# Query and key projections of the last attention from three fp32r products, with a weight load and eight normalisations moved back

## The chip, the cores and the metric

One core of a Trainium2 chip runs the kernel. The metric is the device time of one execution in microseconds (us). A profiled execution also leaves a trace: TensorE (PE for matmuls, PEld for its weight loads), VectorE (DVE), ScalarE (ACT), GpSimd (POOL), SyncE (SP, which here only issues DMAs) and the DMA queues.

## The reference

Four layers of attention and feed-forward work on 2 x 1024 rows of 256 values. The change is in the last attention, in which 1024 + 64 keys per batch (the rows and 64 context rows, both normalised) serve 1024 queries:

```python
xn = layer_norm(x, ln_media_w, ln_media_b)       # 64 context rows
zn = layer_norm(latents, ln_lat_w, ln_lat_b)     # 1024 rows
q = (zn @ Wq)...                                 # 8 heads of 64
kv_in = jnp.concatenate([xn, zn], axis=1)
k = (kv_in @ Wk)...
v = (kv_in @ Wv)...
sim = jnp.einsum('bhqd,bhfd->bhqf', q * scale, k)
alphas = jax.nn.softmax(sim, axis=-1)
out = jnp.einsum('bhqf,bhfd->bhqd', alphas, v)
...
return out @ Wout
```

## The kernel before

The attention (`pe_xattn3`, `act_xattn3`, `dve_xattn3`, `pool_xattn3`, `sp_xattn3`, one function for each engine, each a fixed order written out by hand, with semaphores between them) runs over 16 blocks `G`. A block is one pair of heads and one half (512) of the queries of a batch: batch `G // 8`, pair `G // 2 % 4`, half `G % 2`; keys and values are shared by the two blocks of a pair `n = G // 2`. A block has nine steps `j`, one for each tile of 128 keys (the ninth has the 64 context keys).

In step `j` TensorE makes the scores of tile `j` (four fp32r matmuls: the keys' and queries' high parts, and then both low parts with the negated maxima as one more row), at steps 3, 6 and 8 the products of three tiles with the values (fp32), then a *side*, and last two *rough* tiles of the next block, fp32r scores of which only the row maxima are kept. ScalarE weighs each tile (`act_weigh3`, exp of 128x1024, L2423), GpSimd adds the weights up (`pool_sum3`, 128x1024 from two operands in SBUF, L2470 and L2473), and divides the block before at its step 7 (`pool_divide3`, L2453). VectorE reduces the rough tiles (L2373), makes the reciprocals in quarters (`quarters3`, `dve_divisors3`, L2445; none in block 0), and at step 8 the next block's maxima (`dve_maxima3`, L2378 and two small operations in L2380).

A side is a piece of the preparation of later blocks, all through PSUM bank 7: `q` at step 1 projects the queries of block `G + 2`; `k` at steps 2, 4 and 5 of even blocks projects the keys of the next pair (512, 512 and 64 columns), `v` in odd blocks its values; `s` at step 3 sums the weights over the keys; `m` at step 8 transposes the next block's negated maxima (L2242), and TensorE goes on to the next block behind it; `o` is the output projection. Behind a `q` or `k` side ScalarE copies the result as fp32r high parts (L2280 or L2265, and again for the other half of the partitions), and VectorE subtracts them from PSUM for the low parts (L2302). TensorE's next side waits for those (`s_lo3`), since it writes the same bank.

A rough tile waits until the one two before it has been reduced (`s_ar`). Names: `XT` holds the transposed normalised rows in fp32 (2 x 2048 columns), `x3_CT` the context's, `x3_WQ`, `x3_WK`, `x3_WV` the weights from `oW` on; `XN` is the normalised rows' place from 4096 on, free in the attention until `dve_norm` (L173) fills it with the normalised output, the next stage's input. `s_mi` counts the sides that TensorE has made, `s_mo` what ScalarE has kept, `s_x` finished row tiles, `s_xn` normalised ones. All matmuls are issued by `mm`, L152.

Of the kernel before, what the change touches and what calls it, by code (L numbers as in the profile page):

```python
# [6 lines left out]
ALU = mybir.AluOpType  # L7
# [71 lines left out]
def build(nc, d, out):  # L79
    with ExitStack() as ctx:  # L80
# [2076 lines left out]
        x3_MX, x3_M1, x3_NM = view(o + 15872, 4, 2, 3), view(o + 15896, 4, 2), view(o + 15904, 4, 65)  # L2157
        x3_SM, x3_RC = view(oAW + 3072, 512), view(oAW + 3584, 512)
        x3_OE = [view(oW + 8448 + 1024 * p, 1024) for p in range(3)] + [view(oW + 15360, 1024)]
        s_mi, s_mo, s_lo3 = sem("side_made"), sem("side_kept"), sem("low_parts")  # L2160
        s_one = sem("ones_rows")
        s_am, s_ar = sem("rough_scores"), sem("rough_maxima")
# [46 lines left out]
        def pe_side3(e, s):  # L2209
# [12 lines left out]
            if kind in "kv":  # L2222
                b, p, rows = a // 4, a % 4, 128 if c < 2 else 64
                src = XT[:, :, 1024 * b + 512 * c:1024 * b + 512 * c + 512] if c < 2 else x3_CT[:, :, 64 * b:64 * b + 64]
            if kind == "k":
                n = 512 if c < 2 else 64
                for k in range(2):
                    m = mm(e, psum[:, bk, 0:n], x3_WK[:, k, 128 * p:128 * p + 128], src[:, k, :], k == 0, k == 1)
# [20 lines left out]
            else:  # L2249
                e.wait_ge(s_on, 40 + a + 1 + (c if a == 15 else 0))  # L2250
                for y, t in enumerate(tiles3(a, c)):
                    for p in range(4):
                        m = mm(e, psum[:, bk, 256 * y:256 * y + 256], x3_OE[p][:, 128 * (t % 8):128 * (t % 8) + 128],
                               x3_WO[:, p, :], p == 0, p == 3)
            m.then_inc(s_mi, 1)

        def act_side3(e, s):
            kind, a, c = s
# [215 lines left out]
            m.then_inc(s_pa, 1)  # L2474

        def sp_xattn3(e):
            e.wait_ge(s_xt, 57)
            e.wait_ge(s_x, 96)
            e.dma_start(view(oW + 12288, 3072), d["w3b"][:, 8192:8192 + 3072]).then_inc(s_w3, 16)
            e.wait_ge(s_sc, 48 + 144)  # L2480
            e.dma_start(view(oW + 4096, 4096), d["w3b"][:, 0:4096]).then_inc(s_wm, 16)
            e.wait_ge(s_x, 112)
            e.dma_start(view(oW + 8192, 4096), d["w3b"][:, 4096:8192]).then_inc(s_wm, 16)
# [52 lines left out]
        def act_xattn3(e):  # L2536
            e.wait_ge(s_tp, 57)
            for k in range(2):
                m = e.activation(x3_CT[:, k, :], psum[:, 4, 128 * k:128 * k + 128], ACT.Identity,
                                 bias=sml("mbc")[:, k:k + 1], scale=sml("mwc")[:, k:k + 1])  # L2540
            m.then_inc(s_xt, 1)
            for s in FIRST3[6:]:
                act_side3(e, s)
            for G in range(16):
                for j in range(9):
                    act_weigh3(e, G, j)
                    if j == 8:
                        act_values3(e, G)
                    if side3(G, j):
                        act_side3(e, side3(G, j))  # L2550
                    for i in next_turn3(G, j):
                        act_turn(e, 7, i)
            act_side3(e, ("s", 15, 0))
            for i in range(4, 8):
                act_turn(e, 7, i)

        def dve_xattn3(e):
# [9 lines left out]
            for G in range(16):  # L2567
                for j in range(9):
                    if j == 8 and G + 1 < 16:
                        dve_maxima3(e, G + 1)  # L2570
                    if side3(G, j):
                        dve_side3(e, side3(G, j))
                    if j == 8 and G + 2 < 16:
                        dve_rough3(e, G + 2, 0)
                    if j < 8 and G + 1 < 16:
                        for i in rough_step3(j):
                            dve_rough3(e, G + 1, i)
                    if G:
                        for i in quarters3(G, j):
                            dve_divisors3(e, G - 1, i)  # L2580
                    if (G, j) == (15, 4):
                        dve_divide3(e, 14, slice(0, 512))
                    if G in (9, 11) and 2 <= j <= 5:
                        dve_norm(e, 113 + 2 * (G - 9) + j - 1, 2 * (G - 9) + j - 2)
            dve_side3(e, ("o", 14, 0))
            for t in range(8, 10):
                dve_norm(e, 113 + t + 1, t)
# [527 lines left out]
```

## Time and profile before

| | |
|---|---|
| three timed executions | 1929.12, 1933.93, 1934.39 us, median 1933.93 |
| profiled execution, its time | 1927.72 us |
| span of its instructions | 1925.9 us |
| busy, share of the span | PE 86%, PEld 58%, DVE 56%, ACT 47%, POOL 44% |
| TensorE's granted clock, mean | 0.922 of 2.4 GHz |

The last attention's 16 blocks run from 1208 to about 1720 us of the span. A block with `k` sides takes some 32 us, one with `v` sides some 31.

### The profile page before, as it was taken

To read this page: it belongs to the slowest core of one execution; us is meant where nothing else is said; L and a number is where in the kernel's file an instruction comes from. 1 tells how busy PE (TensorE), PEld (TensorE's weight loads), DVE (VectorE), ACT (ScalarE), POOL (GpSimd) and SP (SyncE) were. 2 spreads that over 40 slices of the span, in tenths; PEclk is the share of its full clock that TensorE was granted. 3 is DMA by queue.
4 is the path that set the end of the run, shared out by engine and by line. 5 is a ranking of instruction groups with operands and counts; after the bars stand their busy time and mean duration, and the time that the engine had idled before them with its cause. 6 is when DMAs were issued, how large, how long until landed. Compare 5 with 4: busy or idle time off the path is not lost.

```text
span 1925.9 us, 26333 instructions
## 1 busy us (share of the span) xinstructions
PE 1652.5 (86%) x9225; PEld 1115.1 (58%) x9225; DVE 1087.6 (56%) x2204; ACT 904.7 (47%) x1502; POOL 851.3 (44%) x802
## 2 busy tenths in 40 slices
PE   5954999969965999974996887999999999997998
PEld 3444999946844333354994665555555655563674
DVE  4662546576866345442446698556655666544335
ACT  2412445513335888742452665555455355431363
POOL 2053221123478455523004474566665666654206
PEclk9776999979987899986998997899999999997999
DMA  9613233030000000062113000000000000012354
GB/s 364 221 58 106 81 137 131 18 117 1 1 21 1 1 7 6 6 263 92 45 50 104 6 1 33 1 1 1 1 1 1 1 1 1 1 44 96 124 169 133
DMA packets 61881, 117.77 MB, mean 61 GB/s; under 512 B 7247, under 2 KB 50499, under 8 KB 59064
## 3 DMA queue, kind: packets, MB, share of 16 engines
q1 hardware_dynamic: 53688, 95.90, 14.2%
q0 software_dynamic: 8064, 20.19, 3.2%
q8 instruction: 77, 1.26, 0.3%
q14 instruction: 52, 0.43, 0.1%
HBM read 72.26 MB, written 44.89 MB: 61 GB/s over the span
## 4 chain that ended last, share of the span: by engine, by line
PE 66%; DVE 12%; POOL 7%; ACT 5%; issue 5%; DMA 4%; SPq 0%; POOLq 0%; ACTq 0%; DVEq 0%
PE psum L152 61%; POOL arena L1815 2%; DMA arena<-xb 2%; ACT arena L1588 2%; DVE arena L2373 2%; POOL arena L856 2%; DVE rounded L2302 2%; POOL arena L1831 1%; POOL xb L1043 1%; DVE arena L157 1%; DVE arena L2445 1%; PE psum L668 1%; DVE arena L1940 1%; DVE arena L173 1%; DVE arena L2380 1%
## 5 line engine op out<-in xcount | busy, mean ns | idle before, releaser
L152 PE MATMUL psum<-arena 128*128 (+16 forms) x5084 | 1034.1, 439 | 106.4 <-DVE arena L1698 21.1
L152 PEld LDWEIGHTS psum<-arena 128*128 128x128 f32 (+4 forms) x5084 | 584.9, 175 | 435.9 <-issue 289.8
L152 PE MATMUL psum<-rounded 128*128 128x256 f32 (+9 forms) x3072 | 547.4, 344 | 14.4 <-ACT arena L1588 5.3
L152 PEld LDWEIGHTS psum<-rounded 128*128 128x128 f32 (+5 forms) x3072 | 408.3, 186 | 172.2 <-issue 63.4
L2473 POOL TENSOR_TENSOR arena<-arena 128x1024 f32<-128x1024 f32 (+1 forms) x111 | 263.2, 2371 | 130.8 <-ACT arena L2423 127.3
L2373 DVE TENSOR_REDUCE arena<-psum 128x1 f32<-128x512 f32 x256 | 163.8, 682 | 98.3 <-PE psum L152 96.8
L2423 ACT ACTIVATE arena<-psum 128x1024 f32<-128x1024 f32 x144 | 147.3, 1024 | 147.8 <-PE psum L152 147.1
L1588 ACT ACTIVATE arena<-psum,arena 128x1024 f32<-128x1024 f32 (+1 forms) x192 | 156.2, 910 | 32.3 <-PE psum L152 32.1
L1831 POOL TENSOR_TENSOR arena<-arena 128x256 f32<-128x256 f32 x128 | 99.4, 803 | 99.5 <-ACT arena L1588 97.8
L856 POOL DMA_INDIRECT arena<-yb,arena x48 | 45.9, 956 | 210.0 <-DMA yb<-arena 196.5
L1196 POOL DMA_INDIRECT yt<-arena x40 | 39.8, 996 | 182.1 <-DVE arena L1159 176.6
L904 DVE SCALAR_TENSOR_TENSOR rounded<-arena,rounded 128x540 fp32r<-128x540 f32 (+1 forms) x96 | 81.8, 885 | 33.4 <-ACT rounded L1105 32.3
L1099 ACT ACTIVATE arena<-psum,arena 128x540 f32<-128x540 f32 x64 | 45.5, 710 | 106.5 <-PE psum L152 103.7
L162 POOL TENSOR_SCALAR arena<-arena 128x1 f32<-128x1 f32 x89 | 22.2, 249 | 146.7 <-DVE arena L158 120.0
L1714 DVE RECIPROCAL arena<-psum 128x512 f32<-128x512 f32 x16 | 53.7, 3358 | 51.4 <-PE psum L152 51.4
L2302 DVE SCALAR_TENSOR_TENSOR rounded<-psum,rounded 64x512 fp32r<-64x512 f32 (+1 forms) x80 | 47.6, 595 | 61.6 <-ACT rounded L2280 32.6
L1790 DVE SCALAR_TENSOR_TENSOR arena<-psum,arena 128x128 f32<-128x128 f32 x92 | 25.9, 344 | 74.5 <-PE psum L152 74.5
L200 ACT ACTIVATE arena<-psum 128x512 f32<-128x512 f32 x48 | 27.1, 596 | 82.8 <-PE psum L192 82.8
L2445 DVE RECIPROCAL arena<-arena 128x128 f32<-128x128 f32 x64 | 58.9, 936 | 11.9 <-ACT arena L2289 11.6
L192 PE MATMUL psum<-arena 128*128 128x128 f32 x192 | 30.9, 300 | 31.9 <-DVE arena L173 29.6
L2470 POOL TENSOR_TENSOR arena<-arena 128x1024 f32<-128x1024 f32 x16 | 38.1, 2382 | 44.9 <-ACT arena L2423 44.9
L1815 POOL TENSOR_TENSOR arena<-arena 128x20 f32<-128x20 f32 x16 | 56.9, 3556 | 1.3
(262 smaller groups left out, 1837.1 us busy)
## 6 DMA issues: line engine op xcount, KB each, us to landing
arena<-in_w SPq DMA_DIRECT2D x8, 2048.0 KB, 8.7
arena<-xb SPq DMA_DIRECT2D x70, 128.0 KB, 2.3
yb<-arena SPq DMA_DIRECT2D x70, 128.0 KB, 1.8
arena<-in_w1u SPq DMA_DIRECT2D x4, 2048.0 KB, 14.0
xb<-arena SPq DMA_DIRECT2D x3, 2048.0 KB, 16.0
xb<-arena SPq DMA_DIRECT2D x2, 2064.0 KB, 31.6
arena<-xb SPq DMA_DIRECT2D x8, 516.0 KB
yt<-arena SPq DMA_DIRECT2D x2, 2048.0 KB, 15.0
```

The costliest lines, as they stand in the source:

```text
L152: return e.matmul(o, l, r, start=start, stop=stop, skip_group_check=True)
L856: e.indirect_dma_start(dst, None, buf, bass.IndirectOffsetOnAxis(idx[:, col:col + 1], 0)).then_inc(s_gth[s], 16)
L904: e.scalar_tensor_tensor(out=dst, in0=src, scalar=1.0, in1=hi, op0=ALU.mult, op1=ALU.subtract).then_inc(sig, 1)
L1588: e.activation(PT[:, u % 3, 2 * h:2 * h + 2, 0:n], psum[:, bk:bk + 2, 0:n], ACT.Exp, bias=NBD[:, 0:1]).then_inc(s_ae, 1)
L1714: settle(e, dve, e.reciprocal(got(c), psum[:, 6 + c % 2, :]))
L1815: e.tensor_tensor(RSH[:, t % 4, :], RSH[:, t % 4, :], cst("nhalf")[:, 0:1].broadcast_to([128, 20]), ALU.pow).then_inc(s_rh, 1)
L1831: e.tensor_tensor(PT[:, u % 3, 2 * h:2 * h + 2, 0:128], PT[:, u % 3, 2 * h:2 * h + 2, 0:128], bc(cst("caus"), 1, 2), ALU.mult).then_inc(s_ ...
L2302: e.scalar_tensor_tensor(out=lo, in0=psum[r, bk, 0:64 if (kind, c) == ("k", 2) else 512], scalar=1.0, in1=hi, op0=ALU.mult, op1=ALU.subtra ...
L2373: m = e.tensor_reduce(x3_MX[:, t, a, c:c + 1], psum[:, bk, :], AX.X, ALU.max)
L2423: e.activation(x3_P[0:rows, g % 4].rearrange("p a n -> p (a n)"), psum[0:rows, bk:bk + 2, :].rearrange("p a n -> p (a n)"), ACT.Exp, scale ...
L2445: e.reciprocal(x3_RC[:, 128 * i:128 * i + 128], x3_SM[:, 128 * i:128 * i + 128]).then_inc(s_rc3, 1)
L2473: m = e.tensor_tensor(ac, ac, x3_P[0:rows, g % 4], ALU.add)
```

## The change

The queries from block 3 on and the keys from pair 2 on are no longer made by fp32 products (two matmul calls, one for each half of the 256 inner values) but by fp32r ones: rows and weights are split into a high part (the value rounded to fp32r) and a low part (the rest), and for each inner half the products high x high, weight high x row low and weight low x row high are summed, six matmul calls. The values stay fp32.

The parts of rows (one batch at a time, 2 x 1024 columns), weights and context are made in the attention: the high ones by ScalarE in steps 5 and 6 of block 0 and step 5 of block 5, the low ones by VectorE in steps 6 and 7 of both blocks. The rows' parts lie in `XN`'s place, the weights' low part over the fp32 weights, the high part where the next stage's weights `w3b[:, 8192:]` were loaded. So that load is issued only after the last `q` side, and the eight `dve_norm` of blocks 9 and 11 stand in blocks 13 and 14.

```diff
+        x3_XH, x3_XL = rview(4096, 2, 1024), rview(4096 + 2048, 2, 1024)
+        x3_WH, x3_WL = rview(oW + 12288, 2, 2, 512), rview(oW, 2, 2, 512)
+        x3_CH, x3_CL = rview(oW + 14336, 2, 128), rview(oW + 14592, 2, 128)
+        s_hi3, s_lw3 = sem("high_parts"), sem("rest_parts")
...
-            if kind == "k":
+            if kind in "kq" and parted3(s):
+                b, p, h = (a // 4, a % 4, c) if kind == "k" else block3(a)
+                n, w = 512 if (kind, c) != ("k", 2) else 64, 1 if kind == "k" else 0
+                e.wait_ge(s_lw3, 5 + 2 * b)
+                hi, lo = (x3_XH, x3_XL) if n == 512 else (x3_CH, x3_CL)
+                rows = slice(512 * h, 512 * h + 512) if n == 512 else slice(64 * b, 64 * b + 64)
+                i = 0
+                for k in range(2):
+                    for wt, x in ((x3_WH, hi), (x3_WH, lo), (x3_WL, hi)):
+                        m = mm(e, psum[:, bk, 0:n], wt[:, w, k, 128 * p:128 * p + 128], x[:, k, rows], i == 0, i == 5)
+                        i += 1
+            elif kind == "k":
...
+        def parted3(s):
+
+            return s[1] >= (3 if s[0] == "q" else 2)
+
+        def act_parts3(e, b):
+
+            if b:
+                e.wait_ge(s_mi, max(SIDE3_AT["q", 7, 0], SIDE3_AT["k", 3, 2]) + 1)
+            else:
+                e.wait_ge(s_xt, 57)
+                e.wait_ge(s_tp, 56)
+            for k in range(2):
+                e.activation(x3_XH[:, k, :], XT[:, k, 1024 * b:1024 * b + 1024], ACT.Copy).then_inc(s_hi3, 1)
+
+        def act_weight_parts3(e):
+            for w in range(2):
+                e.activation(x3_WH[:, w].rearrange("p k n -> p (k n)"), view(oW + 1024 * w, 1024), ACT.Copy).then_inc(s_hi3, 1)
+            e.activation(x3_CH.rearrange("p k n -> p (k n)"), x3_CT.rearrange("p k n -> p (k n)"), ACT.Copy).then_inc(s_hi3, 1)
+
+        def dve_parts3(e, b, k):
+
+            e.wait_ge(s_hi3, 3 + 2 * b + k + 1)
+            if b and k == 0:
+                e.wait_ge(s_mi, max(SIDE3_AT["q", 7, 0], SIDE3_AT["k", 3, 2]) + 1)
+            e.scalar_tensor_tensor(out=x3_XL[:, k, :], in0=XT[:, k, 1024 * b:1024 * b + 1024], scalar=1.0, in1=x3_XH[:, k, :],
+                                   op0=ALU.mult, op1=ALU.subtract).then_inc(s_lw3, 1)
+
+        def dve_weight_parts3(e, w):
+
+            e.wait_ge(s_hi3, w + 1)
+            e.wait_ge(s_mi, max(SIDE3_AT["k", 1, 2], SIDE3_AT["q", 2, 0]) + 1)
+            e.scalar_tensor_tensor(out=x3_WL[:, w].rearrange("p k n -> p (k n)"), in0=view(oW + 1024 * w, 1024), scalar=1.0,
+                                   in1=x3_WH[:, w].rearrange("p k n -> p (k n)"), op0=ALU.mult,
+                                   op1=ALU.subtract).then_inc(s_lw3, 1)
+            if w:
+                e.wait_ge(s_hi3, 3)
+                e.scalar_tensor_tensor(out=x3_CL.rearrange("p k n -> p (k n)"), in0=x3_CT.rearrange("p k n -> p (k n)"),
+                                       scalar=1.0, in1=x3_CH.rearrange("p k n -> p (k n)"), op0=ALU.mult,
+                                       op1=ALU.subtract).then_inc(s_lw3, 1)
...
         def sp_xattn3(e):
-            e.wait_ge(s_xt, 57)
-            e.wait_ge(s_x, 96)
+            e.wait_ge(s_mi, max(SIDE3_AT["q", 15, 0], SIDE3_AT["k", 7, 2]) + 1)
             e.dma_start(view(oW + 12288, 3072), d["w3b"][:, 8192:8192 + 3072]).then_inc(s_w3, 16)
...
+                    if (G, j) in ((0, 6), (5, 5)):
+                        act_parts3(e, G // 5)
+                    if (G, j) == (0, 5):
+                        act_weight_parts3(e)
...
-                    if G in (9, 11) and 2 <= j <= 5:
-                        dve_norm(e, 113 + 2 * (G - 9) + j - 1, 2 * (G - 9) + j - 2)
+                    if G in (0, 5) and j in (6, 7):
+                        dve_parts3(e, G // 5, j - 6)
+                    if G == 0 and j in (6, 7):
+                        dve_weight_parts3(e, j - 6)
+                    if G in (13, 14) and 4 <= j <= 7:
+                        if (G, j) == (13, 4):
+                            e.wait_ge(s_mi, max(SIDE3_AT["q", 15, 0], SIDE3_AT["k", 7, 2]) + 1)
+                        dve_norm(e, 113 + 4 * (G - 13) + j - 3, 4 * (G - 13) + j - 4)
```

## Rows read from the trace of the kernel before

**Rows 1.** Page, part 4: the chain that ended last, by engine.

```profile
PE 66%; DVE 12%; POOL 7%; ACT 5%; issue 5%; DMA 4%; SPq 0%; POOLq 0%; ACTq 0%; DVEq 0%
```

**Rows 2.** Table by stretch, block 5: us, busy PE, PEld, DVE, ACT, POOL, clock, DMA, GB/s.

```profile
1367.00:1398.00 31.00, 30.09 (x149) 18.08 (x149) 17.85 (x28) 14.49 (x19) 20.32 (x11) 1.00 0.00 1
```

**Rows 3.** The chain in order of time behind a query side: start, us, what.

```profile
1309.80 0.60 ACT rounded L2280
1310.43 0.68 DVE rounded L2302
1311.14 0.70 DVE rounded L2302
```

**Rows 4.** Timeline of PEld, fp32 side, then fp32r run: start, us, count, idle before.

```profile
1244.88 0.19 PEld L152 LDWEIGHTS psum<-arena 128*128 128x128 f32 x1
1245.31 0.19 PEld L152 LDWEIGHTS psum<-arena 128*128 128x128 f32 x1 [0.24 <-issue]
...
1242.78 1.82 PEld L152 LDWEIGHTS psum<-rounded 65*128 65x128 f32 x8
```

**Rows 5.** Timeline at step 5 of block 0: the 64-column key side.

```profile
1229.65 0.66 PE L152 MATMUL psum<-arena 128*128 128x64 f32 x4 [0.74 <-DVE rounded L2302]
...
1230.37 0.19 PEld L152 LDWEIGHTS psum<-rounded 128*128 128x128 f32 x1 [0.20 <-DVE arena L2373]
```

**Rows 6.** Timeline of steps 5 to 8 of block 0.

```profile
1231.49 0.54 ACT L2269 ACTIVATE rounded<-rounded 64x64 fp32r<-64x64 f32 x2
1232.43 1.03 ACT L2423 ACTIVATE arena<-psum 128x1024 f32<-128x1024 f32 x1 [0.41 <-PE psum L152]
...
1235.59 2.67 DVE L2373 TENSOR_REDUCE arena<-psum 128x1 f32<-128x512 f32 x4 [2.54 <-PE psum L152]
...
1237.85 4.85 POOL L2473 TENSOR_TENSOR arena<-arena 128x1024 f32<-128x1024 f32 x2 [1.76 <-ACT arena L2423]
...
1238.51 1.81 DVE L2380 TENSOR_SCALAR arena<-arena 128x4 f32<-128x4 f32 x2
...
1241.17 0.65 PE L2242 MATMUL psum<-arena 128*65 128x128 f32 x4
```

**Rows 7.** Groups by form, whole span: count, busy us, mean ns, idle before.

```profile
L901 ACT ACTIVATE rounded<-arena 128x1024 fp32r<-128x1024 f32 x32 | 32.8, 1061 | 0.0
...
L904 DVE SCALAR_TENSOR_TENSOR rounded<-arena,rounded 128x1024 fp32r<-128x1024 f32 x32 | 38.1, 1216 | 0.0
```

**Rows 8.** Timelines, ends of blocks 5 and 14.

```profile
1393.21 0.94 DVE L2445 RECIPROCAL arena<-arena 128x128 f32<-128x128 f32 x1
...
1394.27 2.36 POOL L2473 TENSOR_TENSOR arena<-arena 128x1024 f32<-128x1024 f32 x1 [1.57 <-ACT arena L2423]
...
1395.54 1.19 DVE L2380 TENSOR_SCALAR arena<-arena 128x4 f32<-128x4 f32 x2
...
1397.58 0.54 PE L2242 MATMUL psum<-arena 128*65 128x128 f32 x3
...
1681.39 7.40 POOL L2473 TENSOR_TENSOR arena<-arena 128x1024 f32<-128x1024 f32 x3
...
1690.46 0.62 PE L2242 MATMUL psum<-arena 128*65 128x128 f32 x4 [0.85 <-DVE arena L2380]
```

**Rows 9.** One line's instructions: ns least/median/most, first and last start.

```profile
L173 DVE TENSOR_SCALAR arena<-arena x10: 315/410/448, 1513.1 to 1719.8; 128x256 f32<-128x256 f32 x10
...
L2380 DVE TENSOR_SCALAR arena<-arena x32: 157/395/1736, 1206.1 to 1689.1; 128x4 f32<-128x4 f32 x32
...
L1719 DVE SCALAR_TENSOR_TENSOR arena<-arena x16: 692/1225/1293, 652.6 to 839.9; 128x512 f32<-128x512 f32 x16
```

**Rows 10.** Table by stretch, slow stretches (columns as rows 2).

```profile
1204.25:1214.50 10.25, 8.07 (x26) 6.58 (x26) 5.09 (x10) 2.13 (x3) 3.41 (x3) 0.50 0.01 2
...
1501.20:1504.60 3.40, 3.40 (x11) 2.82 (x11) 1.40 (x3) 1.04 (x2) 2.90 (x7) 0.50 0.00 0
```

**Rows 11.** DMA issues: KB each, median us from issue to landing.

```profile
arena<-in_w3b SPq DMA_DIRECT2D x1, 1536.0 KB, 6.2
```

## The prediction

> **What bounds the kernel now.** I read the chain that ended last first: TensorE carries two thirds of the span [rows 1], so a change in the last attention is worth what it takes off or adds to TensorE's own order of work there. Then the table by stretch: in a block TensorE is busy 30.1 of 31 us at full clock, VectorE, ScalarE and GpSimd between 14.5 and 20.3 [rows 2]. TensorE sets the pace, and the others have 11 to 16 us of room per block as a sum. Room as a sum is not room at every point, so third I read the chain and the timeline through a block. TensorE waits at two kinds of place. After a query or key side it waits for ScalarE's copy (0.60) and VectorE's two low parts (0.68, 0.70) before it may reuse bank 7: 0.73 us of idle [rows 3]. And at step 8 it must transpose the negated maxima (`m`), which VectorE makes last in the block. That second place has almost no room: in block 0 VectorE ends the maxima at 1240.32 and TensorE comes at 1241.17 [rows 6]; in block 5 at 1396.73 against 1397.58 [rows 8]; in block 14 TensorE already waits 0.85 us [rows 8].
>
> **What the parts give.** Thirteen `q` sides (blocks 3 to 15) and twelve 512-column `k` sides (pairs 2 to 7) change from two fp32 products to six fp32r ones; six 64-column `k` sides likewise. An fp32 product shows as two matmuls, and their weight loads start 0.43 us apart (1244.88, 1245.31): four of them are 1.72 us. Eight fp32r weight loads beside 512-column matmuls last 1.82 us, so (1.82 - 0.19)/7 = 0.233 us apart [rows 4]; six are 1.40. The side gets 0.32 us shorter, and since the copy and the low parts follow its end, the 0.73 us of idle stays and the gain passes on: 25 x 0.32 = **-8.0 us**. The Trainium skill (FP8 and Floating Point Precision, TensorE Precision Notes) has true fp32 in 4 passes; with one pass for each fp32r product that would be 4 against 3 passes of the same length, 1.72 to 1.29, and 25 x 0.43 = -10.8 us as an estimate from that page; the weight-load spacing above, 0.233 and not 0.215, speaks against the full step, and I take the measured one.
>
> The 64-column sides get longer: four fp32 matmuls last 0.66 us in all, at a spacing of about 0.11, and six end 0.22 us later. But behind them TensorE waits for VectorE's reductions anyway, until 1230.37, where the four ended their issue at about 1230.15 [rows 5]. So 0; if that cover is gone, 6 x 0.22 = +1.3.
>
> **What the making of the parts costs.** Prices: ScalarE 128x1024 to fp32r 1.06 us, VectorE 128x1024 from two SBUF operands 1.22 [rows 7]; the context's 256 columns I put at 0.4 and 0.5. Per half of the rows 2.1 us on ScalarE and 2.4 on VectorE; for weights and context 2.1 + 0.4 and 2.4 + 0.5. As sums they fit in the room. Their place is steps 5 to 7 of blocks 0 and 5, directly ahead of the maxima in VectorE's queue. There they meet GpSimd: it adds up the weights in 128x1024 operations of 2.37 us. A tiny VectorE operation on SBUF (128x4) takes 0.16 us, but 1.74 at worst; that is the one in block 0 which starts at 1238.51 while GpSimd's sum is under way [rows 6, 9]. L1719, with two SBUF operands, takes 0.69 at least and 1.23 in the median, beside a busy GpSimd [rows 9]. I conclude that such an operation waits for the GpSimd operation under way, and the next GpSimd operation for it.
>
> *Block 0.* ScalarE is free at 1232.03, makes the weights' and the context's high parts until 1234.6, so exp 6 (from 1232.43 before) ends at 1235.6, the rows' high parts at 1236.7 and 1237.7, exp 7 at 1238.7, exp 8 at 1239.8. These delays alone cost TensorE nothing: its last values before `m`, at 1241.17, need exp 8, and take about 1 us [rows 6]. GpSimd sums exp 6 from 1235.7 to 1238.1. VectorE has reduced two of its four tiles at 1236.9, waits for GpSimd until 1238.1, makes rows part 1 until 1239.3; GpSimd's next sum runs to 1241.7; weights part 1 to 1242.9, two reductions to 1244.2, during which GpSimd's last sum starts and runs to 1245.2; then rows part 2, weights part 2 and context, 2.9 us, to 1248.1, the maxima 0.5: 1248.6. TensorE stands at `m` from 1241.17, and behind it in its queue stand the scores of block 1, so ScalarE and GpSimd run dry too: **+7.4 us**. TensorE's own new wait, for the parts at `q` 3, stands behind this one (the maxima come after all parts in VectorE's queue) and is never the last. Without any wait for GpSimd VectorE would end at 1243.7: +2.5, the lower bound.
>
> *Block 5.* ScalarE's two high parts push exp 6 back by some 1.1 us, which nobody waits for. No weights, but one reciprocal at step 6 ends at 1394.15; rows part 1 starts just before GpSimd's sum (1394.27) and ends at 1395.4, reductions 1396.7, GpSimd's sum 1395.4 to 1397.7, rows part 2 to 1398.9, then GpSimd's division (1.26) has the turn to 1400.2 and the maxima end at about 1400.4, against 1397.58 when TensorE comes [rows 8]: **+2.8**; 0.6 without the waits, 5.2 if another sum comes between.
>
> *The norms.* Each is 0.41 us [rows 9], eight of them. In blocks 9 and 11 they stood at steps 2 to 5, where VectorE had room: taking them away gives 0. Block 13 has block 5's pattern, so on block 5's clock [rows 8]: the norm of step 6 goes ahead of the sum, which then runs to 1396.9, the norm of step 7 behind it to 1397.2, the division to 1398.5 and the maxima to 1398.8, against 1397.58: **+1.2**, 0 at the least. In block 14 three sums follow each other without a pause from 1681.39 (7.40 us) [rows 8]; the norm of step 6 is ready at 1686.9 and waits to 1688.8, the last reductions end at 1690.1, the reciprocal at 1691.1, norm and division at 1692.7, the maxima at 1692.9 instead of 1690.31: **+2.5**, 0.7 at the least. They are still in time for the next stage's transposes.
>
> *The clock.* After the halts ahead of block 0 TensorE's granted clock was 0.50 (1.2 GHz) for 10.25 us, and for 3.4 us at the end of block 8 [rows 10]. In such a stretch TensorE does half the work: 3.4 us cost 1.7, and the 10.25 us, with 8.07 busy, some 4. For the halt in block 0 I take 2.3 (bounds 0 and 4), for block 5 0.8 (0 to 1.7), nothing for the shorter ones in 13 and 14: **+3.1**.
>
> *The weight load.* 1536 KB landed in 6.2 us [rows 11]; now it is issued after `q` 15, early in block 13 and over 60 us before the attention's end, behind which its reader, the next stage, starts. On SP's queue only the two loads behind it follow, and they wait for the end of the attention. 0; if it were late, up to 6.
>
> **Sum.** -8.0 + 7.4 + 2.8 + 1.2 + 2.5 + 3.1 = **+9.0 us**. Against the profiled execution, 1925.9 of span and 1.8 around it, that is 1934.9 and 1936.7. The profiled execution was 6.2 below the median of the three runs (1933.93); I add the 9.0 to the median: **1942.9**. Less than 0.3%, 5.8 us, I count as no change.
>
> **Rivals.**
> 1. *The parts don't meet GpSimd* (0.25). VectorE's new operations run at their own length beside the sums. For it: L1719's median is some half a us over its least, not two; against it, GpSimd's operations beside L1719 are short, and the 1.74 us is plain. Then -8.0 + 2.5 + 0.6 + 0 + 0.7 + 0.8 = -3.4: 1930.5, no change. The Trainium skill (SBUF — State Buffer, Who interferes with whom) has it that whoever of the two starts first holds a shared port pair for the whole instruction, also against a VectorE operation with two SBUF inputs; by that rule, with which the 1.74 us agrees, this rival would fall.
> 2. *The maxima are hardly late, and the gain stands: faster* (0.14). Place: step 8 of blocks 0 and 5. If VectorE drains its reductions, which are spaced by TensorE's matmuls, in the gaps, and the maxima come under 2.2 us late over all four blocks, the gain of 8.0 beats 5.8; with 1 us in all, -7.0: 1926.9. If the six products ran at 0.215, -10.8 and it holds up to 5 us of lateness. Against it: block 0 alone has 2.5 us at the least, on durations that are measured.
> 3. *More turns are lost* (0.16). At blocks 5 and 13 the second of the maxima's two small operations loses to GpSimd's last sum, 2.4 us each, and the clock stays low longer after block 0 (+1.7): +9.0 + 6.5 = 1949.4. For it: in block 14 exactly that second operation lasted until the division's end.
>
> **How the numbers follow.** Main case 0.45, rivals 0.25, 0.14, 0.16. The main case's own range, from the bounds of the halts and the clock, is +4 to +13: 1938 to 1947, with 0.06 of its chance below +5.8. Slower: 0.39 + 0.16 = 0.55. No change: 0.06 and 0.22 of rival 1 = 0.28. Faster: rival 2's 0.14 and 0.03 of rival 1 = 0.17. The range takes in rival 1 and most of rival 3, and leaves out rival 2: 1928 to 1950.
>
> **What would show it.** In the changed kernel's profile: six matmuls a side at 0.23 us; side to next side 0.3 us shorter in odd and even blocks; VectorE's new operations in blocks 0 and 5 longer than 1.22 us, and ending with GpSimd's sums; TensorE idle at `m` by some 7 us in block 0, 3 in block 5, 1 to 3 in 13 and 14; a granted clock of 0.5 after block 0. If `m` of block 1 comes within 3 us of its old place, rival 1 is right; if the sides don't shorten, the first term is wrong.

## The result, and the profile after

| | kernel before | changed kernel |
|---|---|---|
| median, us (8 runs each) | 1928.55 (1924.53 to 1934.39) | 1942.19 (1937.54 to 1944.45) |
| profiled execution, its time and span | 1927.72, 1925.9 | 1937.65, 1935.8 |
| mean granted clock | 0.922 | 0.917 |
| attention, first `m` to last `m` | 1206.88 to 1690.46: 483.6 | 1203.51 to 1700.20: 496.7 |

The ratio is 1.0069, 95% interval 1.0054 to 1.0085: slower by some 13 us (10 to 16). Three executions of the whole series, 6 to 30% longer at a lower granted clock, count in no ratio. The attention alone became 13.1 us longer. The span grew by 9.9 only, because this execution came to the attention 3.4 us earlier than the one before did; the change touches nothing there. It is also among the two shortest of the changed kernel's eight, with a mean granted clock of 0.917 where the other seven have 0.913 to 0.915, so a usual execution may spend some us more at half speed than the one read here.

The chain by engine, against [rows 1]: TensorE lost two points and VectorE won two, so more of the end is set by waits for VectorE.

```profile
PE 64%; DVE 14%; POOL 7%; issue 5%; ACT 5%; DMA 4%; SPq 0%; POOLq 0%; ACTq 0%; DVEq 0%
```

Where the sides are, the gain is there. The chain behind a query side (start, us, what) has the same lengths as [rows 3]; the 22 fp32r weight loads of a stretch with such a side are 0.225 us apart, against 0.43 for fp32 [rows 4].

```profile
1344.90 0.60 ACT rounded L2335
1345.50 0.02 issue
1345.53 0.68 DVE rounded L2357
1346.21 0.03 issue
1346.24 0.70 DVE rounded L2357
```

```profile
1340.88 4.93 PEld L152 LDWEIGHTS psum<-rounded 128*128 128x128 f32 x22
```

From `m` to `m`, an even block with three such sides is 1.0 us shorter (block 2: 32.59 to 31.55) and an odd one with one side 0.35 (block 3: 30.43 to 30.07). That is 0.33 to 0.35 a side.

The loss of block 0 is in VectorE's and GpSimd's timelines (start, us, engine, line, what; now L2296 and L2303 make low parts, L2428 reduces, L2435 ends the maxima, L2528 is GpSimd's sum):

```profile
1233.61 2.05 DVE L2296 SCALAR_TENSOR_TENSOR rounded<-arena,rounded 128x1024 fp32r<-128x1024 f32 x1
1235.59 3.37 DVE L2303 SCALAR_TENSOR_TENSOR rounded<-arena,rounded 128x1024 fp32r<-128x1024 f32 x1
1238.89 1.28 DVE L2428 TENSOR_REDUCE arena<-psum 128x1 f32<-128x512 f32 x2
1240.09 2.16 DVE L2296 SCALAR_TENSOR_TENSOR rounded<-arena,rounded 128x1024 fp32r<-128x1024 f32 x1
1242.17 1.21 DVE L2303 SCALAR_TENSOR_TENSOR rounded<-arena,rounded 128x1024 fp32r<-128x1024 f32 x1
1243.30 0.41 DVE L2308 SCALAR_TENSOR_TENSOR rounded<-arena,rounded 128x256 fp32r<-128x256 f32 x1
...
1243.84 0.24 DVE L2435 TENSOR_SCALAR arena<-arena 128x4 f32<-128x4 f32 x2
```

```profile
1232.19 2.39 POOL L2528 TENSOR_TENSOR arena<-arena 128x1024 f32<-128x1024 f32 x1 [1.90 <-ACT arena L2478]
1235.00 6.16 POOL L2528 TENSOR_TENSOR arena<-arena 128x1024 f32<-128x1024 f32 x2 [0.41 <-ACT arena L2478]
```

```profile
1244.22 1.09 PE L2257 MATMUL psum<-arena 128*65 128x128 f32 x4 [6.29 <-DVE arena L2435]
...
1403.57 0.62 PE L2257 MATMUL psum<-arena 128*65 128x128 f32 x4 [2.24 <-DVE arena L2435]
...
1700.20 1.09 PE L2257 MATMUL psum<-arena 128*65 128x128 f32 x4 [3.01 <-DVE arena L2435]
```

Read the first two together. GpSimd's sum ends at 1232.19 + 2.39 = 1234.58, and L2296 ends 1.08 us behind that. L2303 starts at 1235.59 and lasts 3.37 us: the next sum has the turn first, for its 2.4 us, though it was ready at 1235.00 only. The second L2296 ends 1.09 us behind the end of the two sums, 1241.16. The last L2303, with no sum beside it, takes 1.21. So one such operation costs 1.1 to 1.2 us plus what is left of a sum, or a whole one; and the sums, two in 6.16 us instead of 4.85 [rows 6], wait as well. In block 5 the same, on a smaller scale, and there GpSimd's division (L2508) is spread over 2.24 us and L2435's two small operations over 1.10:

```profile
1397.75 1.16 DVE L2296 SCALAR_TENSOR_TENSOR rounded<-arena,rounded 128x1024 fp32r<-128x1024 f32 x1
...
1400.02 2.18 DVE L2296 SCALAR_TENSOR_TENSOR rounded<-arena,rounded 128x1024 fp32r<-128x1024 f32 x1
...
1402.33 1.10 DVE L2435 TENSOR_SCALAR arena<-arena 128x4 f32<-128x4 f32 x2
```

```profile
1397.96 3.16 POOL L2528 TENSOR_TENSOR arena<-arena 128x1024 f32<-128x1024 f32 x1 [1.00 <-ACT arena L2478]
1401.09 2.24 POOL L2508 TENSOR_TENSOR arena<-arena 128x512 f32<-128x512 f32 x1
```

In block 14 two of the norms take 2.2 us, beside four sums in a row; a norm alone takes 0.31. TensorE's idle at `m` there went from 0.85 [rows 8] to 3.01:

```profile
1686.80 2.21 DVE L173 TENSOR_SCALAR arena<-arena 128x256 f32<-128x256 f32 x1
...
1694.43 2.13 DVE L173 TENSOR_SCALAR arena<-arena 128x256 f32<-128x256 f32 x1
...
1698.53 0.31 DVE L173 TENSOR_SCALAR arena<-arena 128x256 f32<-128x256 f32 x1
```

```profile
1686.47 9.94 POOL L2528 TENSOR_TENSOR arena<-arena 128x1024 f32<-128x1024 f32 x4 [0.83 <-ACT arena L2478]
```

What the halts don't explain is the clock. Table by stretch (us, busy PE, PEld, DVE, ACT, POOL, clock, DMA, GB/s) for three stretches at 0.50 (1.2 GHz):

```profile
1241.90:1252.10 10.20, 7.88 (x25) 6.75 (x26) 4.82 (x10) 2.39 (x3) 0.00 (x0) 0.50 0.01 2
1405.80:1409.20 3.40, 3.40 (x9) 2.63 (x9) 1.29 (x2) 1.52 (x2) 0.00 (x0) 0.50 0.00 0
1699.30:1706.10 6.80, 5.88 (x15) 4.36 (x16) 1.45 (x3) 2.61 (x3) 2.97 (x2) 0.50 0.00 0
```

The first begins in block 0's halt, as put, the third in block 14's; the second follows block 5's. Four more of 3.4 us, at 1426.3, 1439.9, 1491.1 and 1511.6, stand in blocks 6 to 9, where no halt is new; in these blocks there was one before, at 1501.2 [rows 10].

All of it by blocks (change in length from `m` to `m`, us; halt is how much later `m` comes for want of the maxima, of which 6.3, 2.24, 0.51 and 2.16 show as new idle at `m`; clock is what is left when 0.33 to 0.35 a side and the halt are taken off):

| block | change | sides | halt | clock | at 0.50, before and after |
|---|---|---|---|---|---|
| 0 | +6.4 | 0 | +6.3 | +0.1 | 7.6, 10.0 |
| 1 | +3.3 | -0.35 | | +3.7 | 0, 8.0 |
| 2, 3, 4 | -2.4 | -2.35 | | 0 | 0, 0 |
| 5 | +2.0 | -0.35 | +2.35 | 0 | 0, 0 |
| 6 | +2.2 | -1.0 | | +3.2 | 0, 6.8 |
| 7 | +1.2 | -0.35 | | +1.6 | 0, 3.4 |
| 8 | +0.6 | -1.0 | | +1.6 | 0, 3.4 |
| 9 to 12 | -2.6 | -2.7 | | 0 | 3.4, 3.4 |
| 13 | +0.3 | -0.35 | +0.6 | 0 | 0, 0 |
| 14 | +2.1 | 0 | +2.1 | 0 | 0, 0.9 |
| sum | +13.1 | -8.4 | +11.4 | +10.2 | |

### The profile page after: what moved, and what is told of

Read it like the earlier page. It is cut to its first block, busy times and chain, and to the rows that moved or that the text cites. A ratio compares the mean times of both kernels' runs of the same rounds, so it can differ in the third digit from the quotient of the medians.

```text
span 1935.8 us, 26493 instructions
## 1 busy us (share of the span) xinstructions
PE 1652.5 (85%) x9287; PEld 1131.8 (58%) x9287; DVE 1102.0 (57%) x2211; ACT 910.8 (47%) x1509; POOL 856.2 (44%) x802
## 4 chain that ended last, share of the span: by engine, by line
PE 64%; DVE 14%; POOL 7%; issue 5%; ACT 5%; DMA 4%; SPq 0%; POOLq 0%; ACTq 0%; DVEq 0%
PE psum L152 60%; DVE arena L2428 2%; ACT arena L1588 2%; POOL arena L1815 2%; DMA arena<-xb 2%; POOL arena L856 2%; DVE rounded L2357 2%; POOL xb L1043 1%; POOL arena L1831 1%; DVE arena L157 1%; DVE arena L173 1%; DVE arena L2500 1%; DVE arena L2435 1%; PE psum L668 1%; DVE arena L1940 1%
## 5 line engine op out<-in xcount | busy, mean ns | idle before, releaser
L152 PE MATMUL psum<-arena 128*128 128x128 f32 (+13 forms) x4960 | 980.7, 435 | 96.1 <-DVE arena L1698 18.8
L152 PEld LDWEIGHTS psum<-arena 128*128 128x128 f32 (+3 forms) x4960 | 562.6, 174 | 406.9 <-issue 280.0
L152 PE MATMUL psum<-rounded 128*128 128x270 f32 (+9 forms) x3258 | 581.9, 345 | 23.2 <-DVE rounded L2357 8.8
L152 PEld LDWEIGHTS psum<-rounded 128*128 128x128 f32 (+3 forms) x3258 | 446.4, 188 | 182.9 <-ACT arena L1588 56.1
L2528 POOL TENSOR_TENSOR arena<-arena 128x1024 f32<-128x1024 f32 (+1 forms) x111 | 265.1, 2388 | 127.2 <-ACT arena L2478 124.2
L2428 DVE TENSOR_REDUCE arena<-psum 128x1 f32<-128x512 f32 x256 | 164.0, 683 | 100.3 <-PE psum L152 98.8
L2478 ACT ACTIVATE arena<-psum 128x1024 f32<-128x1024 f32 x144 | 147.3, 1024 | 150.7 <-PE psum L152 150.0
L173 DVE TENSOR_SCALAR arena<-arena 128x256 f32<-128x256 f32 x128 | 54.7, 449 | 7.1 <-POOL arena L169 3.5
```

What stands on the lines that cost most here:

```text
L152: return e.matmul(o, l, r, start=start, stop=stop, skip_group_check=True)
L173: e.tensor_scalar(xn(t), src(t), MV[:, t, 0:1], RS[:, t:t + 1], ALU.subtract, ALU.mult).then_inc(s_xn, 1)
L2428: m = e.tensor_reduce(x3_MX[:, t, a, c:c + 1], psum[:, bk, :], AX.X, ALU.max)
L2478: e.activation(x3_P[0:rows, g % 4].rearrange("p a n -> p (a n)"), psum[0:rows, bk:bk + 2, :].rearrange("p a n -> p (a n)"), ACT.Exp, scale ...
L2528: m = e.tensor_tensor(ac, ac, x3_P[0:rows, g % 4], ALU.add)
```

## The experiments

The ratio of each is to runs of the kernel before on the same chip. Two chips of three (the runs from `e5_spread` to `e8_fp32_short`, and the last two) take some 280 us instead of 236 behind the attention in every profile taken there, and the kernel before has medians of 1973.05 and 1972.4 on them; so times are compared by ratios, and blocks by their own lengths. Lines of code are cut to the core.

### The norms alone

```diff
-                    if G in (9, 11) and 2 <= j <= 5:
-                        dve_norm(...)
+                    if G in (13, 14) and 4 <= j <= 7:
+                        dve_norm(...)
```

> The kernel before, with only the eight normalisations moved from blocks 9 and 11 to steps 4 to 7 of blocks 13 and 14. Theory A (whatever delays the maxima delays TensorE, and VectorE's operations on SBUF wait for GpSimd's sums): block 13 longer by 0.6 us, block 14 by 2.1, as in the changed kernel; the time +2.7 us, ratio 1.0014. Theory B (the normalisations are hidden, blocks 13 and 14 of the changed kernel are longer for another reason): 0.0.

Measured: 1.0023 (1.0010 to 1.0036). Block 13 +0.56, block 14 +2.13, every other block 0.0. The stretch at 0.50 behind block 14 is 6.8 us long instead of 3.4, and what follows the last `m` took 1.4 more, 236.8 us for 235.4. So the norms cost 2.7 us of halt in their new places. Whether the 1.4 goes with the longer stretch isn't shown: the changed kernel has the same 6.8 us there and takes 235.6 behind it, and `e9_spread_again`, with 3.4, takes 236.0.

### The parts without the new products

```diff
-                    for wt, x in ((x3_WH, hi), (x3_WH, lo), (x3_WL, hi)): ...
+                    m = mm(e, psum[:, bk, 0:n], wf[:, w, k, ...], xf[:, k, :], k == 0, k == 1)
```

> The changed kernel with all parts made, at their places and with their waits, but the query and key sides back to fp32 products of the unsplit rows and weights (the weights' low part is written over their high part, so that the fp32 weights stay). Theory A (halts from the making of the parts, and the slower clock in blocks 1 and 6 to 8 follows from them): the halts stay, 6.3 us in block 0 and 2.2 in block 5, slow clock behind them stays, and the 8 us of the sides are given back: before +19 to +21 us, ratio 1.0100 to 1.0109. Theory C (the slow clock of blocks 6 to 8 comes from the fp32r sides themselves): halts stay, no slow clock in blocks 6 to 8, before +15, ratio 1.0077.

Measured: 1.0090 (1.0070 to 1.0110). Blocks 0, 1, 5, 13 and 14 got longer by 6.38, 3.68, 2.33, 0.58 and 2.13; the others kept their lengths, but for block 9, which lost its stretch at 0.50. TensorE's idle at `m` is that of the changed kernel (6.29 there):

```profile
1246.19 1.09 PE L2256 MATMUL psum<-arena 128*65 128x128 f32 x4 [6.30 <-DVE arena L2434]
```

So the making of the parts with the norms costs 15.1 us in these blocks, 11.4 of it a later `m`, whatever product reads them. The ratio can't tell theory A from theory C, since its interval is 13.5 to 21.2 us; the attention of the profiled execution, 13.5 longer, is on the side of C. What surprised: with all the halts, nothing in blocks 2 to 13 ran at 0.50, though TensorE idled 2.24 us at the end of block 5 as in the changed kernel.

### The products without the low parts

```diff
-                e.wait_ge(s_lw3, 5 + 2 * b)
+                e.wait_ge(s_hi3, 5 + 2 * b)
...
-                    for wt, x in ((x3_WH, hi), (x3_WH, lo), (x3_WL, hi)):
+                    for wt, x in ((x3_WH, hi), (x3_WH, hi), (x3_WH, hi)):
...
-                        dve_parts3(e, G // 5, j - 6)
-                        dve_weight_parts3(e, j - 6)
```

> The changed kernel without the low parts: VectorE makes none of them, and the six products of a side read the high parts in their place; the high parts, the late load and the moved normalisations stay. Theory A: no halt in blocks 0 and 5, so no slow clock behind them; -8.0 us from the sides, +2.7 from the normalisations: before -5.3 us, ratio 0.9972. Theory C (slow clock from the fp32r sides): slow stretches in blocks 6 to 8 stay at 6.4 us of loss, before +1, ratio 1.0006.

Measured: 0.9993 (0.9981 to 1.0005). No halt in blocks 0 and 5; even blocks -1.0, odd ones -0.35, as in the changed kernel. ScalarE's high parts cost TensorE nothing. But block 4 has a new stretch at 0.50 (1352.6), 1.6 us: -8.4 + 2.7 + 1.6 = -4.1, and the attention is 3.8 shorter. The ratio gives -1.3 (-3.7 to +1.0). That shuts out theory A's -5.3 and comes near theory C's +1; but the stretches that C put in blocks 6 to 8 didn't come, only the one in block 4.

### GpSimd's sums cut where the parts stand

```diff
+            if G in (0, 5) and j >= 6:
+                e.tensor_tensor(ac[:, :, 0:1], ac[:, :, 0:1], x3_P[0:rows, g % 4, :, 0:1], ALU.add)
```

> The changed kernel with GpSimd's sums at steps 6, 7 and 8 of blocks 0 and 5 cut to one column (left out but for that; a 1 is added to the sums of these two blocks so that their reciprocals stay finite). Theory A (VectorE's operations with two SBUF operands wait for GpSimd's): each takes its own 1.2 us, the halt in block 0 falls from 6.3 us to about 2.5, the one in block 5 from 2.2 to at most 0.3; with less slow clock behind them the time falls from the changed kernel's before +13.4 to about before +4, ratio 1.0020. Theory D (the number of VectorE's operations alone makes the lateness): the halts stay, ratio 1.0069.

Measured: 1.0053 (1.0035 to 1.0070). VectorE's same operations in block 0, with nothing long beside them on GpSimd, and TensorE behind them:

```profile
1239.99 1.23 DVE L2296 SCALAR_TENSOR_TENSOR rounded<-arena,rounded 128x1024 fp32r<-128x1024 f32 x1
1241.13 1.22 DVE L2303 SCALAR_TENSOR_TENSOR rounded<-arena,rounded 128x1024 fp32r<-128x1024 f32 x1
...
1243.47 1.21 DVE L2296 SCALAR_TENSOR_TENSOR rounded<-arena,rounded 128x1024 fp32r<-128x1024 f32 x1
```

```profile
1246.66 0.62 PE L2257 MATMUL psum<-arena 128*65 128x128 f32 x4 [2.35 <-DVE arena L2438]
```

That is the mechanism: each operation is back at 1.22 us, the halt of block 0 falls from 6.29 to 2.35 (the lower bound of the prediction was 2.5), that of block 5 from 2.24 to 0.46. The 2.35 that is left is the length of the added work itself ahead of the maxima. The time missed the expectation all the same: eight stretches of 3.4 us at 0.50 (1248.3, 1299.5, 1313.2, 1364.4, 1565.7, 1579.4, 1630.6, 1644.3), none of them in blocks 0 and 5, and only the first behind one of these two. This pointed away from the halts as the cause of the clock.

### The parts spread over earlier steps

```diff
+        PARTS_AT3 = {
+            (0, 3): lambda e: (dve_parts3(e, 0, 0), dve_context_part3(e)),
+            (1, 2): lambda e: dve_parts3(e, 0, 1),
+            (1, 3): lambda e: dve_weight_parts3(e, 0),
+            (1, 4): lambda e: dve_weight_parts3(e, 1),
+            (5, 3): lambda e: dve_parts3(e, 1, 0),
+            (5, 4): lambda e: dve_parts3(e, 1, 1)}
...
+                    if G == 13 and 2 <= j <= 5: (norms 0 to 3)
+                    if G == 15 and j < 2: (norms 4 to 7)
```

`q` 3 stays an fp32 side here, since its parts come later; ScalarE makes its parts at steps 2, 3, 5 and 6 of block 0 and 2 and 3 of block 5.

> The changed kernel with the making of the parts and the normalisations spread: VectorE makes one part a step, at steps 3 of block 0, 2 to 4 of block 1 and 3 and 4 of block 5, where TensorE's step is long (query 3 therefore stays fp32, 24 long sides instead of 25), and the normalisations stand at steps 2 to 5 of block 13 and 0 and 1 of block 15. Theory A (only the place ahead of the maxima costs): no halt, no slow clock behind one, -7.7 us, ratio 0.9960. Theory C (fp32r sides bring slow stretches of their own, some 4 us, as the kernel with products only suggests): -3.7 us, ratio 0.9981. If the parts cost wherever they stand: not below 1.0000.

Measured: 1.0008 (0.9997 to 1.0019). Blocks 1, 5, 13 and 14 are late no more (+0.03, -0.28, -0.31, -0.01). Block 0 is 5.0 longer: VectorE at step 3 and TensorE behind it.

```profile
1226.24 2.62 DVE L2296 SCALAR_TENSOR_TENSOR rounded<-arena,rounded 128x1024 fp32r<-128x1024 f32 x1
1228.78 2.57 DVE L2309 SCALAR_TENSOR_TENSOR rounded<-arena,rounded 128x256 fp32r<-128x256 f32 x1
1231.27 1.40 DVE L2358 SCALAR_TENSOR_TENSOR rounded<-psum,rounded 64x512 fp32r<-64x512 f32 x2
```

```profile
1232.72 1.11 PE L152 MATMUL psum<-arena 128*128 128x64 f32 x4 [3.58 <-DVE rounded L2358]
```

The context's part is 0.41 us of work (L2308 above) and took 2.57, a sum of GpSimd's ahead of it. The rows' part ahead of it had lost a turn too, 2.62 us for 1.2. Both stood ahead of step 4's key side's low parts (L2358), and TensorE waited 3.58 us instead of 0.73 for them: 2.85 of the 5.0 us. The rest came with 6.8 us at 0.50 from 1231.8 on. The ratio is where the third expectation had it, but not for its reason: the other parts cost nothing in their places. So room counts up to the next thing that TensorE needs from VectorE, which is a side's low parts as well as `m`.

### The narrow key side one step later, in both kernels

```diff
-            if j in (2, 4, 5) and n + 1 < 8:
-                return ("v" if G % 2 else "k", n + 1, (2, 4, 5).index(j))
+            at = (2, 4, 5) if G % 2 or G == 8 else (2, 4, 6)
+            if j in at and n + 1 < 8:
+                return ("v" if G % 2 else "k", n + 1, at.index(j))
```

In the spread kernel, and in the kernel before:

> The spread kernel, with the 64-column key side at step 6 instead of 5 in blocks 0, 2, 4, 6, 10 and 12. Between the key side of step 4 and this one TensorE then has work, so its 0.73 us of idle at step 5 goes; the narrow side's low parts (0.47 us) come nearer to the maxima. Theory C1 (that idle is what the slow stretches start from, which in the changed kernel begin some 21 us into even blocks): they go too; -1.6 to -4.4 us for the idle and -4 for the clock, ratio 0.9931 to 0.9952. Theory C2 (they have nothing to do with this idle): ratio of the spread kernel less 0.0008 to 0.0023.

> The kernel before with only the 64-column key side at step 6 instead of 5 in six even blocks. No slow stretches there in the kernel before, so the idle alone: -1.6 us (0.73 less 0.47 in each of six blocks) to -4.4 us, ratio 0.9977 to 0.9992.

Measured: 1.0063 (1.0045 to 1.0082) and 1.0064 (1.0049 to 1.0080). Both missed. Block 2 of the second:

```profile
1297.35 2.00 PE L152 MATMUL psum<-rounded 128*128 128x512 f32 x5 [1.46 <-DVE arena L2374]
```

```profile
1298.80:1302.20 3.40, 3.40 (x9) 1.02 (x9) 1.34 (x2) 1.02 (x1) 3.03 (x2) 0.50 0.00 0
```

Ahead of step 5's first rough tile TensorE now idles 1.46 us instead of 0.73: the tile waits for VectorE's reductions, which stand behind the low parts, and the narrow side had been done in that time for nothing. A block with 1.46 lost 1.0 us where the clock held, and 2.6 with a stretch at 0.50 behind it, as here and in blocks 4, 10 and 12. So stretches come in a kernel of fp32 sides as well when these idles are longer. This is the cover that the prediction named for the 64-column sides, seen from its other side.

### An fp32 side as short as the new one

```diff
-                    m = mm(e, psum[:, bk, 0:n], x3_WK[...], src[:, k, :], k == 0, k == 1)
+                    w = 320 if n == 512 and a >= 2 and k else n
+                    m = mm(e, psum[:, bk, 0:w], x3_WK[...], src[:, k, 0:w], k == 0, k == 1)
```

and the same for `q`, in the kernel before. 192 of the 512 columns lack their second product, so this kernel only shows what a shorter side is worth.

> The kernel before, fp32, with the second product of each query side from 3 on and of each long key side from pair 2 on cut to 320 of 512 columns (the rest of that product is left out), which makes a side 1.39 us, as long as six fp32r products. No parts, no moved operations. Theory C3 (slow stretches come with the kind of the products): none in blocks 2 to 8 and 10 to 13, -8.0 us, ratio 0.9958. Theory C4 (they come with the shorter blocks, at another beat): slow stretches there as in the kernel with products only, -4 us, ratio 0.9979.

Measured: 0.9962 (0.9948 to 0.9975), the first clear gain of the series. Even blocks -0.98, odd ones -0.3, and one stretch at 0.50 in blocks 1 to 13 (1628.2, where theory C3 had none). Block 9 has lost its stretch and block 13 has one instead, so the attention's 8.0 us are the sides alone: shorter sides are worth their full 8 us when the products remain fp32.

### The spread kernel, mended, and the changed kernel again

```diff
-            (0, 3): lambda e: (dve_parts3(e, 0, 0), dve_context_part3(e)),
-            (1, 2): lambda e: dve_parts3(e, 0, 1),
+            (0, 6): lambda e: dve_parts3(e, 0, 0),
+            (1, 2): lambda e: (dve_parts3(e, 0, 1), dve_context_part3(e)),
```

(ScalarE's weight parts move to steps 2 and 3 of block 1.) `e10_changed_again` is the changed kernel beside it on the same chip.

> The spread kernel with block 0 mended: there VectorE's rows part and context part at step 3 waited for GpSimd and made the low parts of the key side of step 4 late (3.6 us of idle). Now block 0 has one part, at step 6, and no high part of ScalarE's between; the context's part stands at step 2 of block 1. Theory A: block 0 as long as before, all other blocks as in the spread kernel, -5 us against that kernel's ratio of 1.0008, and less slow clock: ratio 0.997, -4 to -7.7 us. If a part at step 6 of block 0 already makes the maxima late: block 0 longer by 1 to 3 us, ratio 0.998 to 1.000.

> The changed kernel once more, beside the others of this call on their chip. Ratio 1.0069 as before, in its earlier interval of 1.0054 to 1.0085; halts of 6.3 us in block 0 and 2.2 in block 5. Theory C (slow stretches come with the fp32r sides): at least one in blocks 6 to 13 that follows no halt over 1.5 us.

Measured: 0.9997 (0.9982 to 1.0013) and 1.0086 (1.0068 to 1.0105). The mended kernel has no new halt: blocks 0, 1, 5, 13 and 14 changed by +0.08, +0.03, -0.34, -0.33 and 0.00, and the attention takes 480.4 us instead of 483.6. It is 3.2 shorter and not 7.7, because of stretches at 0.50 in blocks 4, 7 and 8 besides the one of block 9. So the blocks came as theory A had them, but the ratio of 0.997 was missed by the clock. The changed kernel, whose ratio came out at the upper end of its first interval, repeated its halts (6.31, 2.25, 3.01) and had 17 us at 0.50 in blocks 2 to 13, not at the same places as the first time (1358.9, 1403.3 for 6.8, 1427.2, 1509.1); two of them, 1427.2 and 1509.1, follow no halt, as its theory C asked.

### What the clock goes by: the kind of product, or the low parts

Both start from the mended kernel. The first makes all parts, and its sides are the short fp32 ones; the second makes no low parts, and its sides are six fp32r products.

```diff
+                for k in range(2):
+                    y = 320 if n == 512 and k else n
+                    m = mm(e, psum[:, bk, 0:y], wf[:, w, k, ...], xf[:, k, 0:y], k == 0, k == 1)
```

```diff
-                    for wt, x in ((x3_WH, hi), (x3_WH, lo), (x3_WL, hi)):
+                    for wt, x in ((x3_WH, hi), (x3_WH, hi), (x3_WH, hi)):
...
-                        PARTS_AT3[G, j](e)
```

> The mended spread kernel with all parts made at the same places, but the query and key sides fp32 again, the second product of each long side cut to 320 of 512 columns (the rest of it left out; the weights' low part is written over their high part): a side as long as six fp32r products, all else the same. Theory C3 (the slow stretches that ate the gain come with fp32r products): none or one in blocks 2 to 13, -7.0 us or more, ratio 0.9955 to 0.9965. Theory C5 (they come with the making of the parts, or with the beat of the blocks): as the mended spread kernel, ratio 0.9997, its interval 0.9982 to 1.0013.

> The mended spread kernel without the low parts: VectorE makes none, all six fp32r products of a side read high parts; the normalisations stand at their hidden places. Theory C3: slow stretches as in the mended spread kernel, three or so of 3.4 us in blocks 2 to 13, ratio 0.9975 to 1.0000. If only the making of the low parts brings them: ratio 0.9955 to 0.9965.

Measured: 0.9964 (0.9948 to 0.9980) and 0.9981 (0.9964 to 0.9997). Blocks 2 to 13 of four kernels in the table by stretch (columns as above, the clock third from the end), in the order `e8_fp32_short`, `e11_spread_fp32_short`, then `e9_spread_again`, `e12_spread_high_only`:

```profile
1272.05:1658.36 386.31, 365.75 (x1651) 213.40 (x1649) 242.53 (x392) 203.67 (x282) 248.33 (x125) 1.00 0.00 1
```

```profile
1267.02:1653.36 386.34, 365.75 (x1651) 213.45 (x1649) 243.64 (x390) 205.42 (x284) 249.92 (x125) 1.00 0.01 5
```

```profile
1268.99:1659.76 390.77, 370.49 (x1711) 225.66 (x1709) 243.55 (x390) 205.42 (x284) 249.86 (x125) 0.98 0.01 5
```

```profile
1268.76:1659.69 390.93, 370.62 (x1710) 225.75 (x1709) 241.47 (x388) 205.44 (x284) 248.16 (x125) 0.98 0.01 5
```

With fp32 sides 386.3, with fp32r sides 390.8 or 390.9, and low parts or none make no difference. The 4.5 us are the clock: 3.4 us at 0.50 in the first two, 13.6 in the last two, which have their stretches at the same four places (1351.9, 1427.0, 1478.2, 1498.6 and 1351.6, 1426.7, 1477.9, 1498.4). The 10.2 us more at half speed cost 4.5. Both expectations of C3 were met. What these runs hold apart is the sides from all the rest, and not the type of the product from the number of products: with fp32r sides the same blocks have 60 matmuls and 60 weight loads more (1711 for 1651, 1709 for 1649), and no run has as many fp32 ones.

Over all the profiled executions, one of each kernel, us at 0.50 in blocks 2 to 13:

| sides | kernels | us |
|---|---|---|
| fp32 | before, e1, e2, e8, e11 | 3.4, 3.4, 0, 3.4, 3.4 |
| fp32r | changed, e3, e4, e5, e9, e10, e12 | 17, 6.8, 23.8, 10.2, 13.6, 17, 13.6 |
| narrow side moved | e6 (fp32r), e7 (fp32) | 20.4, 13.6 |

## Why the prediction was right, and where its sum was off

The time forecast, 1942.9, was met (1942.19), and the forecast of slower too. The difference was forecast as +9.0 and is +13.6 of the medians, +13.1 of the attention. That the level came out to 0.7 us is luck, for two errors met: the median of three that I added to was 5.4 us above the one of eight, 1933.93 against 1928.55, and the sum was some 4.5 too small.

- **The sides, -8.0**: -8.4 measured, 0.33 to 0.35 a side where 0.32 was put, with a spacing of 0.225 for 0.233. The step was right, and the idle behind a side stayed at 0.73. The estimate of -10.8 from the 4 passes that the Trainium skill (FP8 and Floating Point Precision, TensorE Precision Notes) has for true fp32, with fp32r products 0.215 apart, didn't come true: they are 0.225 apart. The 64-column sides cost nothing, as put.
- **Block 0, +7.4**: 6.3, in the order of the working: rows part 1 behind one sum, weights part 1 behind the whole next one (3.37 us), rows part 2 behind the last, the rest free at 1.21. The us between is in the small steps; ScalarE's parts took 1.0 us each, not 1.06, so GpSimd's sums started earlier.
- **Block 5, +2.8**: 2.35, with the division ahead of the maxima, as put.
- **The norms, +1.2 and +2.5**: 0.6 and 2.1 in blocks 13 and 14; `e1_norms_moved` has them alone, with the same 0.56 and 2.13.
- **The weight load, 0**: it landed in 5.9 us and nobody waited.
- **The clock, +3.1**: this is the term that was mis-sized; it measured +10. I had put 2.3 for block 0's halt and 0.8 for block 5's, and nothing elsewhere. Block 0's halt cost 3.8 (10.2 us at 0.50, within my bound of 4), and the same 10.2 us stand there in `e2_parts_only` and `e10_changed_again`. The stretch behind block 5's halt cost 1.6, but that the halt made it isn't shown: with the same idle `e2_parts_only` has none there, and `e10_changed_again` 6.8 us. Another 4.8 come from stretches in blocks 6 to 8 that follow no new halt. My upper bound of the difference, +13, fell just short of what came, and was as near only because the halts came in 2.5 under their terms. Nor is +4 to +13 what my bounds add up to: with every term at its lower bound the sum is -4.2, with every term at its upper one +14.0.

Rival 1, that the parts don't meet GpSimd, falls by the rows of block 0 and by `e4_sums_cut`: the same operations take 1.22 us when the sums are cut. The Trainium skill (SBUF — State Buffer, Who interferes with whom) says that the first of the two to start holds the port pair that they share for the whole instruction and the other blocks fully. The trace agrees where L2296 ends 1.08 and 1.09 us behind a sum's end. Rival 2 falls with 6.3 us of halt in block 0 alone. Rival 3 would have had its extra turns at blocks 5 and 13, where none was lost; the part of it that spoke of a clock low for longer was nearest to what came.

What is shown: of block 0's halt of 6.3 us, 3.9 come from VectorE's SBUF operations and GpSimd's sums taking turns (cutting the sums removes them) and 2.35 from the added work itself; for the norms in blocks 13 and 14 the turns are read from the timeline only. The halts go away when the parts are spread and kept clear of a side's low parts (`e9_spread_again`). Then the change is worth between -3.4 and +2.5 us by its ratio, -3.2 in the profiled attention, and not -8, because of the clock (`e9` against `e11`, which differ in the sides' products alone, and by 1.5 us for each stretch; their chips differ, but `e12`, on the chip of `e11`, has the blocks of `e9`). What stays open is why fp32r sides bring the low clock, and whether it is the type or the number of the products. All that the rows give is the place: in every profile each stretch at 0.50 in blocks 1 to 13 starts 0.5 to 2.6 us behind an idle of TensorE of 0.73 us or more, mostly some 21 us into an even block or 1.5 us into an odd one. Of such idles blocks 2 to 13 have 25, in the kernel before as in `e9` and `e11`, 7 to 14 us apart (once some 20) and then, in each pair of blocks, 30 us without one; the kernel before and `e11` have a stretch behind one of the 25, `e9` behind four. The two chips' ratios of `e9` and `e12`, which have the same blocks, are 0.9997 and 0.9981, so the end effect of the stretches in unprofiled runs is known to some 3 us only. None of the kernels that leave nothing out is shown to be faster than the one before.

## What to carry to other kernels

Room on VectorE is to be counted from one deadline to the next (here a side's low parts, and `m`), and an operation with SBUF operands beside GpSimd's can cost its own length plus nearly one whole GpSimd instruction, even when it is 0.4 us long (here 2.57). Work that looks like the last of a block should be put behind the deadline rather than ahead of it: the same parts and norms that cost 11.4 us of halts brought none when spread. And a saving in TensorE's own work should be measured together with the granted clock of the stretch, since more than half of this one (4.5 of 7.7 us in the profiled executions) went there, without a halt of its own.

## What the runs showed of the hardware

- Of two VectorE operations in a row, the second can lose its turn to a GpSimd operation that became ready while the first ran or waited: 3.37 us for an operation of 1.21.
- A VectorE operation with one tensor operand in SBUF is caught as well: the norms (128x256) took 2.21 and 2.13 us beside the sums, 0.31 alone.
- About a halt of 6.3 us the clock was at 0.50 for 10.2 us, in three executions of three, and about one of 3.58 for 6.8. Behind an idle of 2.24 or 2.25 at the same place it was there for 3.4, 0 and 6.8 us in three executions.
- Behind idles of 0.73 us too, the clock fell for 3.4 us now and then: with the narrow key side at its old place, 0 to 3.4 us in all over blocks 2 to 13 with fp32 sides and 6.8 to 23.8 with fp32r sides, where the busy times of TensorE differ by the clock only (370 of 391 us, 366 of 386). A stretch of 3.4 us costs some 1.6.
